# Softmax sums of three attention layers inverted with tokens on partitions, and a new table for the order of the steps

## What is computed

```
# layer 0: 16 heads, a window of 32 tokens
weights = jax.nn.softmax(logits, axis=-1)
out = jnp.einsum('bntd,bntde->bnte', weights, val_win)
# layer 1: 8 local heads over 512 tokens, 8 global heads over 128 groups of 4 tokens, causal
att = jax.nn.softmax(scores, axis=-1)
return jnp.einsum('bhqk,bhkd->bhqd', att, v)
# layer 3: 16 heads over 512 tokens, then a norm of each head's output
weights = jax.nn.softmax(scores, axis=-1)
out = jnp.einsum('bhts,bhsk->bhtk', weights, v)
norms = jnp.linalg.norm(out, axis=-1)
```

## Time and profile before

| | |
|---|---|
| median of three runs | 3785.52 us (3783.11 to 3786.83) |
| the profiled execution | 3781.06 us, span from first to last instruction 3779.3 us |
| granted TensorE clock, mean | 0.884 of full speed |
| busy: TensorE, VectorE, ScalarE, GpSimd | 81%, 64%, 44%, 16% of the span |
| chain that ended last, by engine | TensorE 52%, VectorE 28%, transfers 6%, ScalarE 5%, issue 5% |

### The profile page before, as it was taken

The page is one execution under the profiler, slowest core; times in us unless marked ns, Lnnn a source line. Parts: engine busy times, 40 slices in busy tenths (PEclk is TensorE's granted clock), DMA queues, the critical chain, the costliest instruction groups (busy, mean ns, idle before and its releaser), DMA issues.

```text
span 3779.3 us, 43414 instructions
## 1 busy us (share of the span) xinstructions
PE 3062.2 (81%) x15958; PEld 1536.6 (41%) x16050; DVE 2423.9 (64%) x4577; ACT 1666.3 (44%) x2467; POOL 597.1 (16%) x425
## 2 busy tenths in 40 slices
PE   5468869997799868998589976998679986898579
PEld 1124423553245432554235532454325542355225
DVE  7435876568756775668755686557765687552635
ACT  5314615464245534456154652456344561542143
POOL 2001101311023010321013110230103210130113
PEclk7568869998799979998899987999799987998799
DMA  3530275312842066502753028420565127531344
GB/s 114 62 111 9 53 137 135 104 26 74 141 145 69 21 112 131 151 28 53 136 135 104 24 73 143 144 72 20 111 119 161 32 51 139 131 105 36 75 131 126
DMA packets 331157, 353.80 MB, mean 94 GB/s; under 512 B 98433, under 2 KB 264129, under 8 KB 329345
## 3 DMA queue, kind: packets, MB, share of 16 engines
q1 hardware_dynamic: 330945, 351.02, 40.2%
HBM read 301.70 MB, written 48.61 MB: 93 GB/s over the span
## 4 chain that ended last, share of the span: by engine, by line
PE 52%; DVE 28%; DMA 6%; ACT 5%; issue 5%; POOL 2%; SPq 2%; ACTq 0%; DVEq 0%; POOLq 0%
DVE MX L1613 7%; PE PS L1824 6%; PE PS L1847 6%; PE PS L1851 5%; PE PS L1678 5%; PE PS L1686 5%; PE PS L1111 3%; DVE U L897 3%; PE PS L1792 3%; DMA UU<-k_scratch 3%; DVE U L904 3%; PE PS L1803 2%; DVE D L1667 2%; DVE D L956 1%; POOL D L1419 1%
## 5 line engine op out<-in xcount | busy, mean ns | idle before, releaser
L1419 POOL TENSOR_TENSOR D<-D,GW 128x512 f32<-128x512 f32 x320 | 435.1, 1361 | 1412.6 <-ACT D L1492 1177.5
L787 ACT ACTIVATE U<-U 128x2048 f32<-128x2048 f32 x256 | 487.9, 1909 | 180.5 <-DVE U L897 98.4
L1662 DVE SCALAR_TENSOR_TENSOR D<-D,PS 128x512 f32<-128x512 f32 x336 | 229.0, 681 | 402.3 <-ACT D L1496 284.6
L1492 ACT ACTIVATE D<-PS 128x512 f32<-128x512 f32 x336 | 200.0, 595 | 614.8 <-PE PS L1847 614.8
L1824 PEld LDWEIGHTS PS<-WST,D 128*128 128x128 f32 (+1 forms) x2688 | 354.6, 199 | 165.3 <-DVE D L1667 95.5
L1824 PE MATMUL PS<-WST,D 128*128 128x128 f32 (+1 forms) x2688 | 381.9, 287 | 30.5 <-DVE D L1667 30.5
L1851 PE MATMUL PS<-XT,WST 128*128 128x512 f32 (+1 forms) x672 | 373.3, 638 | 27.4 <-DVE D L1662 26.0
L904 DVE SCALAR_TENSOR_TENSOR U<-PP,RD,QB 128x512 f32<-128x512 f32 x512 | 361.8, 772 | 47.5 <-ACT QB L784 28.7
L1111 PE MATMUL PS<-U,resident 128*32 128x512 f32 x2048 | 303.7, 673 | 102.5 <-ACT U L787 102.5
L1847 PE MATMUL PS<-XT,WST 128*128 128x512 f32 (+1 forms) x672 | 370.2, 634 | 8.5 <-DMA WST<-in_pairs_dram 4.3
L1613 DVE TENSOR_REDUCE MX<-PS 128x2 f32<-128x1024 f32 x256 | 297.9, 1219 | 88.1 <-PE PS L1770 88.1
(11 more groups left out here) (356 smaller groups left out, 3822.0 us busy)
## 6 DMA issues: line engine op xcount, KB each, us to landing
GW<-gates_scratch SPq DMA_DIRECT2D x320, 256.0 KB, 4.4
WST<-in_pairs_dram SPq DMA_DIRECT2D x336, 192.0 KB, 2.4
U<-band_scratch SPq DMA_DIRECT2D x32, 1280.0 KB, 15.3
UU<-in_w_dram SPq DMA_DIRECT2D x64, 512.0 KB, 7.2
UU<-pad_scratch SPq DMA_DIRECT2D x8, 1792.0 KB
UU<-q_scratch SPq DMA_DIRECT2D x24, 384.0 KB
UU<-k_scratch SPq DMA_DIRECT2D x24, 384.0 KB
e_scratch<-D SPq DMA_DIRECT2D x8, 1024.0 KB, 4.5
```

Source lines behind the costliest of these rows:

```text
L787: e.activation(ring(i), ring(i), ACT.Gelu).then_inc(S["act"], 1)
L1419: e.tensor_tensor(AV[:, n % 3, :], AV[:, n % 3, :], GW[:, p // 2 % GWS, p % 2, :], ALU.mult).then_inc(S["gated"], 1)
```

## The change

In all three layers the sums are taken with tokens on partitions: `OS` is the stationary operand and eight columns of `sel_den` (`den_rows`, one of each group of 16) move, so that 512 tokens and 16 heads give 128 partitions x 64 values. VectorE inverts these 64 values, spreads each over 16 columns with a copy (`over_rows`), and TensorE brings that back to channels on partitions by products with the identity, into PSUM, from where the multiplication reads. The TensorE steps of layers 0 and 1 now hold both kinds of product with a wait on VectorE (`rden`) between them; in layer 3 the small products stand where L1812 stood, the identity products at pairs 3 and 5, and the multiplications at pairs 4 and 6, each over half. The numbers of steps are the same. The table `STARTS` is new in all its entries, `TURN` is unchanged. The core of the diff, without the table:

```
@@ a_dve, layer 0
             e.wait_ge(S["den"], at("den", b, 1))
+            step(e, e.reciprocal(RT[:, :, :, :], PS(2)[:, 0:16 * NT].rearrange("p (j h g) -> p j h g", j=NT, h=2)))
+            yield
             for h in range(2):
-                last = e.reciprocal(RCA[:, h, :], PS(2 + h))
...
-            e.tensor_tensor(OS[:, :, :], OS[:, :, :], RCA[:, :, :], ALU.mult).then_inc(S["on"], 1)
+                e.tensor_copy(rows_of(RCA[:, h, :], NT), over_rows(RT[:, :, h, :], NT)).then_inc(S["rden"], 1)
+            yield
+            e.wait_ge(S["den"], at("den", b, 2))
+            e.tensor_tensor(OS[:, :, :], OS[:, :, :], PSall[:, 2:4, :], ALU.mult).then_inc(S["on"], 1)
@@ a_dve, layer 1
-            e.wait_ge(S["den"], at("den", b, 2))
-            e.reciprocal(RCA[:, 1, 0:P], PS(1)[:, 0:P])
-            yield
-            step(e, e.reciprocal(RCA[:, 0, :], PS(0)))
-            yield
+            e.wait_ge(S["den"], at("den", b, 3))
+            e.reciprocal(RT[:, :, 0, :], PS(0)[:, 0:8 * NT].rearrange("p (j g) -> p j g", j=NT))
+            step(e, e.reciprocal(RT[:, 0, 1, :], PS(0)[:, 8 * NT:8 * NT + 8]))
+            yield
+            e.tensor_copy(rows_of(RCA[:, 1, 0:P], 1), over_rows(RT[:, 0:1, 1, :], 1))
+            e.tensor_copy(rows_of(RCA[:, 0, :], NT), over_rows(RT[:, :, 0, :], NT)).then_inc(S["rden"], 1)
+            yield
+            e.wait_ge(S["den"], at("den", b, 4))
@@ a_pe, layer 0
             e.wait_ge(S["os"], at("os", b, 1))
+            for j in range(NT):
+                for h in range(2):
+                    last = e.matmul(PS(2)[:, 16 * j + 8 * h:16 * j + 8 * h + 8], OS[:, h, P * j:P * j + P], den_rows,
+                                    start=(j == 0 and h == 0), stop=(j == NT - 1 and h == 1), skip_group_check=True)
+            last.then_inc(S["den"], 1)
             for h in range(2):
-                last = e.matmul(PS(2 + h), cn("sel_den"), OS[:, h, :], start=True, stop=True)
+                e.wait_ge(S["rden"], at("rden", b, h + 1))
+                for j in range(NT):
+                    last = e.matmul(PS(2 + h)[:, P * j:P * j + P], RCA[:, h, P * j:P * j + P], ident, start=(j == 0), stop=(j == NT - 1), skip_group_check=True)
             last.then_inc(S["den"], 1)
@@ a_pe, layer 1: five small products, e.wait_ge(S["rden"], at("rden", b, 3)), five identity products
...
@@ b_dve_pairs, layer 3
-                    e.wait_ge(S["den3"], at("den3", b, h + 1))
-                    e.reciprocal(RC[:, h, :], PZ(2)).then_inc(S["nrm3"], 1)
+                    e.wait_ge(S["den3"], at("den3", b, 1 + p // 4))
+                    if p == 1:
+                        step(e, e.reciprocal(RT3, PZ(2)[:, 0:16 * NT].rearrange("p (j h g) -> p j h g", j=NT, h=2)))
+                        e.tensor_copy(rows_of(RC[:, 0, :], NT), over_rows(RT3[:, :, 0, :], NT))
+                        e.tensor_copy(rows_of(RC[:, 1, :], NT), over_rows(RT3[:, :, 1, :], NT)).then_inc(S["nrm3"], 1)
+                    else:
+                        e.tensor_tensor(OS3[:, 0, :], OS3[:, 0, :], PZ(2), ALU.mult).then_inc(S["nrm3"], 1)
                 if l == 3 and p == 6:
...
-                    e.tensor_tensor(OS3[:, :, :], OS3[:, :, :], RC, ALU.mult).then_inc(S["nrm3"], 1)
+                    e.tensor_tensor(OS3[:, 1, :], OS3[:, 1, :], PZ(2), ALU.mult).then_inc(S["nrm3"], 1)
@@ b_pe_pairs, layer 3
-                if l == 3 and p == 3:
...
+                if l == 3 and p in (3, 5):
+                    if p == 3:
+                        yield
+                    h = p // 4
+                    e.wait_ge(S["nrm3"], at("nrm3", b, h + 1))
+                    for j in range(NT):
+                        last = e.matmul(PZ(2)[:, P * j:P * j + P], RC[:, h, P * j:P * j + P], ident, start=(j == 0), stop=(j == NT - 1), skip_group_check=True)
+                    last.then_inc(S["den3"], 1)
```

Of the table, as an example, the first entries of `a_pe` before and after:

```
-        15.68, 17.61, 22.37, 22.37, 25.45, 36.40, 42.11, 45.92, 51.63, 54.47, 58.30, 61.15, 61.15, 63.04, 66.84, 69.68,
+        9.964, 11.176, 11.176, 16.606, 20.960, 53.019, 74.470, 74.470, 74.470, 74.470, 77.865, 77.865, 77.865, 77.865, 77.865, 78.481,
```

More of the change, by code:

```diff
@@ L423, in build @@
         MXA = sb("MXA", [P, NT, NH])
+        RT = sb("RT", [P, NT, 2, 8])
         NMF = sb("NMF", [P, NT, NH])
@@ L455, in build @@
         MX3 = sb("MX3", [P, NT, NH])
+        RT3 = MX3[:, :, :].rearrange("p j (h g) -> p j h g", h=2)
         NMF3 = sb("NMF3", [P, NT, NH])
@@ L954, in a_dve @@
             e.wait_ge(S["den"], at("den", b, 1))
+            step(e, e.reciprocal(RT[:, :, :, :], PS(2)[:, 0:16 * NT].rearrange("p (j h g) -> p j h g", j=NT, h=2)))
+            yield
             for h in range(2):
-                last = e.reciprocal(RCA[:, h, :], PS(2 + h))
-                if h == 0:
-                    yield
-            step(e, last)
+                e.tensor_copy(rows_of(RCA[:, h, :], NT), over_rows(RT[:, :, h, :], NT)).then_inc(S["rden"], 1)
             yield
-            e.tensor_tensor(OS[:, :, :], OS[:, :, :], RCA[:, :, :], ALU.mult).then_inc(S["on"], 1)
+            e.wait_ge(S["den"], at("den", b, 2))
+            e.tensor_tensor(OS[:, :, :], OS[:, :, :], PSall[:, 2:4, :], ALU.mult).then_inc(S["on"], 1)
             yield
@@ L1271, in a_pe @@
             e.wait_ge(S["os"], at("os", b, 3))
-            e.matmul(PS(0), cn("sel_den"), OS[:, 0, :], start=True, stop=True)
-            e.matmul(PS(1)[:, 0:P], cn("sel_den"), OS[:, 1, 0:P], start=True, stop=True).then_inc(S["den"], 1)
+            for j in range(NT):
+                e.matmul(PS(0)[:, 8 * j:8 * j + 8], OS[:, 0, P * j:P * j + P], den_rows, start=(j == 0), stop=False, skip_group_check=True)
+            e.matmul(PS(0)[:, 8 * NT:8 * NT + 8], OS[:, 1, 0:P], den_rows, start=False, stop=True, skip_group_check=True).then_inc(S["den"], 1)
+            e.wait_ge(S["rden"], at("rden", b, 3))
+            e.matmul(PS(1)[:, 0:P], RCA[:, 1, 0:P], ident, start=True, stop=True)
+            for j in range(NT):
+                last = e.matmul(PS(0)[:, P * j:P * j + P], RCA[:, 0, P * j:P * j + P], ident, start=(j == 0), stop=(j == NT - 1), skip_group_check=True)
+            last.then_inc(S["den"], 1)
             yield
@@ L1811, in b_pe @@
             e.wait_ge(S["os3"], at("os3", b, 2))
-            e.matmul(PZ(2), cn("sel_den"), OS3[:, 0, :], start=True, stop=True).then_inc(S["den3"], 1)
+            for j in range(NT):
+                for h in range(2):
+                    last = e.matmul(PZ(2)[:, 16 * j + 8 * h:16 * j + 8 * h + 8], OS3[:, h, P * j:P * j + P], den_rows,
+                                    start=(j == 0 and h == 0), stop=(j == NT - 1 and h == 1), skip_group_check=True)
+            last.then_inc(S["den3"], 1)
             yield from b_pe_pairs(e, b, 3)
@@ L1831, in b_pe_pairs @@
                 m, w = P if p < npair(l) else 64, WST[:, (PAIRS * b + n) % WS, :, :]
-                if l == 3 and p == 3:
-                    yield
-                    e.wait_ge(S["nrm3"], at("nrm3", b, 1))
-                    e.matmul(PZ(2), cn("sel_den"), OS3[:, 1, :], start=True, stop=True).then_inc(S["den3"], 1)
+                if l == 3 and p in (3, 5):
[3 more added lines that the diff above has]
+                    e.wait_ge(S["nrm3"], at("nrm3", b, h + 1))
+                    for j in range(NT):
+                        last = e.matmul(PZ(2)[:, P * j:P * j + P], RC[:, h, P * j:P * j + P], ident, start=(j == 0), stop=(j == NT - 1), skip_group_check=True)
+                    last.then_inc(S["den3"], 1)
                 if l == 3 and p == 8:
```

22 lines of the change are left out of this document (12 added, 10 removed), and 172 rows, old and new, of the table STARTS.

## The result

Two groups of runs were made of the changed kernel. In the first it takes 3724.84 us (3722.5 to 3727.58) against 3784.32 us of the kernel before on the same chip: a ratio of 0.9843, interval 0.9826 to 0.986, 59 us less. The forecast was 3761.5 us, 24 less. The direction is right, the time lies within the range, and the size is two and a half times too small. On a second chip, beside two of the experiments, the ratio is 0.9806 (0.9792 to 0.982).

The account below looks back on a forecast made before the run. TensorE's own work bounds 258 of 443 us a turn, the order of dependences the other 185. Terms of +2.2, -0.5, -4.2 and -0.5 us a turn, eight times, gave -24 from 3785.5: 3761.5 us, range 3712 to 3808.

Parts of the forecast that it names:

- The prices of single instructions: New instructions: reciprocal of 64 elements 0.57 us, spreading copy 0.42, eight small products 1.9, or 3.9 at the lower clock.
- Layer 0: Layer 0's division: step 7.1 us against 3.7, less 1.2 of waiting; +2.2 us a turn, bounds +0.2 and +4.3.
- upper bound of 9.2 us: Layer 0's division step if the clock stays down throughout and the copies take 0.69 us; +4.3 us a turn.
- Layer 3: Layer 3's division: +1.9 us of TensorE work, -2.4 of gaps; -0.5 us a turn, bounds +1.9 and -1.0.
- bound of -1.0: Layer 3's best case, in us a turn: copies free and the second gap gone too.
- Layer 1: Layer 1's division: -0.6 us from idle time and work, -3.6 from the clock kept; -4.2 a turn, bounds -0.6 and -4.5.
- The table: The new step order of both threads: -0.5 us a turn, ends -7 and +1.1; moves in full stretches give nothing.
- The price of L938: VectorE's subtractions, L933 before the change, now ahead of layer 3's statistics: +1.1 us a turn at most.
- The sum: Layer 0, Layer 3, Layer 1 and the table: 2.2 - 0.5 - 4.2 - 0.5 = -3.0 us a turn, -24 over eight.
- The order gives more: Rival: the table brings -7 us a turn for -0.5, 3709.5 us, more likely 3735; chance 0.22.
- The waits inside the steps: Rival: TensorE stands still in layer 0, the clock falls in layer 1; +4.3 us a turn, 3820, milder 3804; chance 0.23.

Follow-up runs that it names:

- e5_layer3_old: The changed kernel with layer 3's division as before; ratio 0.987 to the kernel before the change.
- e2_table_old_code: The kernel before the change with the new step table and its old code; ratio 0.9928, 27 us less.
- e1: The changed code of all three layers with the step table of the kernel before; ratio 0.9971, 11 us less.
- h1: The changed code with the new order for a's steps up to the last gelu item, the old order behind it; ratio 0.9901 to the kernel before.

## Why the prediction was right or wrong

**The prices of single instructions** held (above), the small products too: those of layer 3 take 1.95 us (L1839 above), for 1.9 forecast. Eight columns (0.12 us a record) cost what sixteen do. So the trace agrees with what the forecast took from the section "LDWEIGHTS (loading the stationary operand)" of the Trainium skill's page "TensorE: Matmul & The Clock Gate", and not with the estimate of 0.4 us for eight products, worked out from its "Back-to-back issue gap" alone.

**Layer 0**, +2.2 us a turn: right in sign and near in size (1.4 on one chip with the new table; some 1.7 across chips with the old one), in part by luck. Two of its steps were wrong and work against each other. The identity products run at the lower clock in all turns (3.78, not 2.05); the upper bound of 9.2 us for the step had that, the chosen value not. And the transfer behind L1806, for which TensorE would wait anyway, takes part of the step for nothing; the forecast looked only at VectorE for what hides the step. That the 1.17 us before the projection goes was right for the old table; under the new one it is gone with the old division too.

**Layer 3**, -0.5: wrong, -2.1 in the stretch with the old table and -3.4 with the new. The step that failed is the size of the gaps. The forecast took 2.4 us for two of them, left 0.4 of the second, and charged 1.9 us of added work in full. With the old table the idle time of the stretch fell by 3.2 us (4.1 to 0.9), since a's score products, too, waited for maxima behind the reciprocals; and the busy time rose by 1.15, not 1.9. The clock is not the reason for that, as it is 1.00 there before and after; the reason was not found. The bound of -1.0 had none of this. By the run's time (e5_layer3_old, 1.3 to 3 us a turn across chips) the part is worth less than the stretch says, and still more than forecast.

**Layer 1**, -4.2: near under the new table (5.2 in the stretch, by the profiles of e2_table_old_code and the changed kernel, of which 2.1 to 3.9 a turn show in the run's time), wrong under the old (1.5 in the stretch), for which it was priced. The term rested on the clock staying up. It stays up in half of the turns. And with the old table even those turns gain only 2.3 us (38.9 to 36.6): the idle time that the gap loses comes back in part at the next wait for VectorE. That a gap of this kind keeps the clock was inferred from two rows; eight turns of the same gap go both ways.

**The table**, -0.5: wrong, and the largest error: -3.4 us a turn by itself (27 / 8). The step that failed is "with no gap to fill, that gives nothing". There were gaps. One is the 2.0 us before L1806, and the merged order showed the band products within two places of it; two places were taken for none. What the move brings there with the old code is 1.7 us, and it comes by the clock of the products behind it. The others are in the stretch held for full, which idled 9.9 us in the kernel before and loses 2.3 of them by the table alone. The price of L938, +1.1 at most, is the 1.1 to 1.3 that was measured. Up to the end of the gelu stretch the order brings 3 us more, half of it idle and half busy time (from a's L1299 to its L1138, right behind that stretch, 22.9 and 174.3 us in e1, 21.0 and 172.5 in h1); which of its moves does that was not found.

**The sum** left out that the parts depend on each other. It priced the new code in the old order and the new order with the old code. Under the new order the long reciprocals of layer 3 stand before maxima that a's scores need, so removing them is worth 3.4 instead of 2.1 us in their stretch; and at layer 1, where a pair's product waited 4.12 us behind them, 5.2 instead of 1.5. These two differences, 5 us a turn or 40 us, are more than the 20 to 35 that neither part had alone, as not all that a stretch gains reaches the end of the turn. That they are the whole of it is an inference: layers 1 and 3 were not run alone in the old order.

**The rivals.** "The order gives more" had the right size (3735 to 3709.5), with the wrong place: it named the idle time of the Vector-bound stretch, which gave 1 to 2 us, and the rest came in the stretches behind it. "The waits inside the steps" was half right: both waits are there as drawn, the identity products of layer 0 are at the lower clock, L938 is in the way. It lost because layer 1's clock did not fall in all turns and layer 3 gave more.

## What to carry to other kernels

When a change brings new code and a new order together, price the code in the new order too: look at what now stands next to each long instruction, and at every single step that changes sides with a wait, even by one place. A long Vector instruction is worth what the waits behind it are, and in a tight order that is more than in a loose one. Where a gap of about a microsecond is left in a full stretch, price the clock both up and down and take the middle, and compare variants on one chip before believing half a per cent.

## What the runs showed of the hardware

The granted clock isn't fixed by the instructions of a stretch and the gap before them. Behind the same gap of 1.11 us the same instructions run at 2.4 GHz throughout in three turns, and in three others for a part at 1.2 (mean 1.00 and 0.95, 33.7 and 35.4 us for the stretch). In layer 3's maxima, 32 reductions that keep VectorE busy for 37 us, the two trace rows of the kernel before show the same stretch at a clock of 0.94 and of 0.65, in 37.4 and in 39.3 us:

```profile
1848.70:1886.05 37.35, 23.72 (x160) 6.63 (x160) 36.74 (x32) 0.59 (x1) 0.00 (x0) 0.94 1.24 159
2290.26:2329.54 39.28, 32.11 (x160) 7.39 (x160) 37.59 (x32) 0.59 (x1) 0.00 (x0) 0.65 1.18 152
```

So in this kernel even a stretch that VectorE bounds is 2 us longer where TensorE's clock is down; VectorE itself is busy 0.85 us longer. The clock isn't all that sets its length: in the changed kernel one of these stretches took 40.05 us at 0.94. And the ratio of one and the same pair of kernels was 0.9843 on one chip and 0.9806 on another, of another pair 0.9757 and 0.9776, where each interval is only ±0.0013 to ±0.0017 wide. Why the chips differ was not tried.
